# Identity matmuls on TensorE in five early waits of a cross-attention and expert-FFN kernel

## What is computed

```python
x = x + xattn(layernorm(x), ctx, pos, pos, Wq, Wkv, Wout, bout)
x = x + ffn(layernorm(x), gate_w, bias, shared_w1, shared_w3, shared_w2, w1, w3, w2)

# xattn: 32 heads of 16
q = (x @ Wq).reshape(b, n, 32, 16)
k, v = split(ctx @ Wkv, 2)
q, k = apply_axial_rope(q, pos), apply_axial_rope(k, pos)
w = softmax(einsum('bqhd,bkhd->bhqk', q, k) * 16 ** -0.5)
return einsum('bhqk,bkhd->bqhd', w, v).reshape(b, n, 512) @ Wout + bout

# ffn: one shared expert, and the best 2 of 16 routed experts, inner width 352
shared = (silu(x @ w1.T) * (x @ w3.T)) @ w2.T
routed = sum over e of combine[:, e] * (silu(x @ w1[e].T) * (x @ w3[e].T)) @ w2[e].T
```

## Time and profile before

| | us |
|---|---|
| three runs | 683.81, 691.29, 691.58 |
| their median | 691.29 |
| profiled execution, first to last instruction | 686.8 |
| TensorE busy in it | 635.5 |

### The profile page before, as it was taken

How to read it: one execution, slowest core, us unless ns; L and a number is a source line. 1 busy time by engine, 2 the same in 40 slices (tenths; PEclk the granted TensorE clock), 3 DMA queues, 4 the chain that set the end, 5 groups by cost and what they waited for, 6 DMA issues and landing times.

```text
span 686.8 us, 19435 instructions
## 1 busy us (share of the span) xinstructions
PE 635.5 (93%) x7104; PEld 406.1 (59%) x7104; DVE 503.7 (73%) x976; ACT 368.5 (54%) x620; POOL 329.9 (48%) x390
## 2 busy tenths in 40 slices
PE   2779999999999999988999999999997999999992
PEld 0255666666666666656566566666664666666661
DVE  8688888888888899866485935676775676666671
ACT  4255655656566665566411115665764666666660
POOL 3434555555555555432000011467666577767562
PEclk9889999999999999999999999999999999999997
DMA  8934755344444445660322563676778855555952
GB/s 291 247 56 62 173 103 94 88 97 99 99 99 99 99 99 122 94 125 33 115 86 76 204 220 92 173 219 98 209 211 257 229 115 92 92 88 150 246 92 33
DMA packets 105296, 90.63 MB, mean 132 GB/s; under 512 B 71649, under 2 KB 75745, under 8 KB 105249
## 3 DMA queue, kind: packets, MB, share of 16 engines
q1 hardware_dynamic: 91872, 60.28, 34.2%
q0 software_dynamic: 8752, 20.71, 16.2%
q10 hardware_dynamic: 4624, 9.00, 4.0%
HBM read 69.85 MB, written 22.81 MB: 135 GB/s over the span
## 4 chain that ended last, share of the span: by engine, by line
PE 76%; DMA 7%; issue 4%; POOL 3%; ACT 3%; DVE 3%; SPq 1%; POOLq 0%; ACTq 0%; DVEq 0%
PE p_sc L725 14%; PE p_qk L694 13%; PE p_sc L694 12%; PE p_qk L505 8%; PE p_v L505 8%; PE p_pv L594 4%; DMA used_twice_too<-used_twice 3%; PE p_pv L597 3%; PE p_tr L688 2%; PE p_pv L712 2%; PE p_sc L553 2%; PE p_pv L604 2%; PE p_sc L574 2%; PE p_sc L577 1%; SPq L426 1%
## 5 line engine op out<-in xcount | busy, mean ns | idle before, releaser
L1088 DVE TENSOR_REDUCE negmax<-p_sc 128x4 f16<-128x512 f32 x128 | 79.4, 683 | 6.8 <-PE p_sc L553 5.4
L934 ACT CAST hiddenT<-p_pv 128x384 f16<-128x384 f32 x54 | 25.8, 478 | 106.0 <-PE p_pv L712 102.2
L812 ACT ACTIVATE prob<-p_sc 128x512 f32<-128x512 f32 x128 | 66.1, 604 | 20.7 <-PE p_sc L577 20.4
L1494 POOL DMA_INDIRECT out<-prob,to_at x38 | 68.2, 1796 | 10.1 <-issue 8.2
L725 PE MATMUL p_sc<-used_twice,hiddenT 128*128 128x512 f16 (+1 forms) x306 | 71.6, 379 | 0.9 <-DVE hiddenT L1218 0.9
L1474 POOL COPY from_at<-from_rows 128x1 uint32 (+1 forms) x40 | 32.3, 808 | 80.8 <-DVE from_rows L1333 77.4
L694 PE MATMUL p_qk<-used_twice,xeT 128*128 128x352 f16 x420 | 68.4, 313 | 0.6 <-DMA xeT<-xn2T_dram 0.6
L694 PE MATMUL p_sc<-used_twice,xeT 128*128 128x352 f16 x420 | 68.4, 312 | 0.0
L1214 DVE TENSOR_TENSOR hidden<-p_sc,act_g 128x352 f32<-128x352 f32 x55 | 28.8, 524 | 52.5 <-PE p_sc L694 32.1
L921 ACT COPY xeT<-p_tr 128x1024 f16<-128x1024 f16 x40 | 40.5, 1012 | 37.2 <-PE p_tr L688 35.6
L505 PE MATMUL p_qk<-used_twice,xnT 128*128 128x512 f16 x192 | 53.1, 405 | 5.3 <-DVE swp L1066 5.3
(11 more groups left out here) (180 smaller groups left out, 1482.3 us busy)
## 6 DMA issues: line engine op xcount, KB each, us to landing
w<-e SPq DMA_DIRECT2D x20, 1408.0 KB
w<-e SPq DMA_DIRECT2D x20, 512.0 KB
out<-stream SPq DMA_DIRECT2D x17, 256.0 KB, 2.0
xn_dram<-xn_parts SPq DMA_DIRECT2D x16, 256.0 KB, 2.2
xn2T_dram<-xn2T SPq DMA_DIRECT2D x16, 256.0 KB, 2.5
w<-e SPq DMA_DIRECT2D x20, 192.0 KB
xeT<-xn2T_dram ACTq DMA_DIRECT2D x14, 256.0 KB, 2.8
stream<-x ACTq DMA_DIRECT2D x1, 3072.0 KB, 16.8
```

The lines of the kernel that those rows point to most:

```text
L812: act.activation(prob[:, c % RING, :], p_scored(c)[:], ACT.Exp, scale=SCALE).then_inc(exp_ready, 1)
L1088: dve.tensor_reduce(negmax[:, c % 2, at:at + CH], p_scored(c)[:].rearrange("p (h t) -> p h t", t=P), AX_X, ALU.max, negate=True).then_inc( ...
L1494: pool.indirect_dma_start(out=out, out_offset=bass.IndirectOffsetOnAxis(ap=to_at[:, par, u:u + 1], axis=0), in_=ye[:, par, u], in_offset=N ...
```

## The change

TensorE gets a helper `keep_busy(n)`, which issues n matmuls with the fp16 identity as the stationary operand and the same identity, repeated four times, as 512 moving columns. They write the whole of `p_pv`, and nothing reads the result. They wait for no semaphore of their own and signal none. Eight of them stand ahead of the very first transposes, behind the wait for `ident_ready`. Others stand at places in the step function that a table `BUSY` names by step and place: 14, 15, 8, 9 and 9. The table is looked up only for steps with a constant number, so the loop's body stays as it was.

```diff
+            def keep_busy(n):
+
+                for _ in range(n):
+                    pe.matmul(p_pv[:], ident16[:], ident16[:].rearrange("p (o t) -> p o t", o=1).broadcast_to([P, CH, P]), start=True, stop=True)
+
+            BUSY = {(0, "before k"): 14, (1, "before q"): 15, (2, "before q"): 8, (2, "before scores"): 9, (3, "before shift"): 9}
+
+            def fill(b, where):
+
+                if isinstance(b, int):
+                    keep_busy(BUSY.get((b, where), 0))
+
             pe.wait_ge(ident_ready, 1)
+            keep_busy(8)
             xn_transpose(0, 0)
...
                 on(-1, project_k, 1)
+                fill(b, "before shift")
                 on(-3, negmax_transpose)
...
+                fill(b, "before q")
                 on(-1, project_q, 0)
                 on(-3, spread_recip, 0)
                 on(-1, project_q, 1)
+                fill(b, "before scores")
                 on(-2, scores, 0)
...
                 on(0, xn_transpose)
+                fill(b, "before k")
                 on(0, project_k, 0)
```

## The result

The change made the kernel slower. Over 20 runs of each, its median is 694.92 us (690.61 to 701.88) against 690.33 us before (683.81 to 694.93). The ratio is 1.0092, 95% interval [1.0065, 1.0118], so some 6 us. The ratios in this document are taken over the fast runs of each kernel, those within 1.5% of its fastest. My forecast was 688.5 us, 2.8 us under the 691.29 us of the three runs known then, and its range ended at 692.

The account below looks back on a forecast made before the run. TensorE, busy 635.5 of 686.8 us, was taken as the bound, so only the start could gain: 1.0 (transposes) + 1.8 (step 2) + 0 (shifted scores) = 2.8 us off the 691.3 median gives 688.5 us, range 681 to 692.

Parts of the forecast that it names:

- The clock: At TensorE's start: the added matmuls raise the clock by 11.3 us, so that q of batch 0 runs fast.
- The case in which the four transposes don't count: Start: transpose-mode work doesn't raise the clock, which rises near 12.4 us; q starts 0.7 us late, the sum loses 0.1.
- What the slow pace cost: Slow matmuls at the start: at most 2.06 us shows for q of batch 0, 1.88 in step 2, shifted scores 0 to 0.9.
- what is late next: After q of batch 0: busy DMA passes on only 1.0 of 2.06 us; step 2 then gives 1.8.
- the transposes' term: DMA transposes of batch 0's q: an earlier q half queues behind k's, so scores gain 1.0 us, between 0 and 2.06.
- that of step 2: Step 2's scores, q half and v chunk at the fast pace: 1.88 us less some 0.1 for row maxima, 1.8.
- The 4.5 us by which I set the median over the profiled execution: Whole kernel: the three-run median 691.3 us lies 4.5 us over the profiled 686.8; if that spread stays, the forecast is 688.5.
- A shift should survive: the order is fixed, and from some 140 us on TensorE is full: Whole kernel behind the start: time gained there, 2.8 us, moves everything later forward and lasts to the end.
- the term for the added matmuls: TensorE's early waits: each added matmul costs 0.215 or 0.427 us; hidden at the fast pace, partly over at the slow.
- The slower one: From q of batch 0 on: identity matmuls don't raise the clock and delay work by 9.3 us, to 700.6 us; chance 0.05.
- Absorbed: Scores still wait for DMA transposes until 31.7; the end moves at most 1 us, to 690.3 to 691.3; chance 0.18.
- The spread's rival: Start: run-to-run spread is the clock's and the change removes it, giving 684.0 us, or 681.0 from the best run; chance 0.20.

Follow-up runs that it names:

- e9: e8 run again unchanged (the change plus 65 matmuls of 16 columns, 128 added in all), against the kernel before: ratio 0.9938, median 684.79 us.
- e10: e8's code with all 128 added matmuls at 16 columns, against the kernel before: ratio 0.9974, median 686.43 us.
- e1: The kernel before once more with no edit, as a second sample against the kernel before: ratio 0.9974.
- e5: The kernel before with 63 matmuls of 16 columns added in TensorE's first wait, against the kernel before: ratio 1.0108.
- e6: The kernel before with 128 matmuls of 16 columns added in TensorE's first wait, against the kernel before: ratio 0.9961.
- e4: The change with only the groups of steps 2 and 3 (8, 9, 9), against the kernel before: ratio 1.0007.
- e2: The change with its 63 added matmuls at 16 columns in place of 512, against the kernel before: ratio 1.0102, median 699.28 us.
- e11: The kernel before with 191 matmuls of 16 columns in its first three waits, against the kernel before: ratio 1.0065.
- e8: The change plus 65 matmuls of 16 columns in its own waits, 128 added in all, against the kernel before: ratio 0.9930, median 686.41 us.
- e3: The change with only the groups ahead of the first transposes, k and q (8, 14, 15), against the kernel before: ratio 1.0027.
- e7: The kernel before with 32 matmuls of 16 columns added in TensorE's first wait, against the kernel before: ratio 1.0012.
- e12: The change plus 33 matmuls of 16 columns in its waits, 96 added in all, against the kernel before: ratio 0.9979.

## Why the prediction was wrong

**The clock, right.** The identity matmuls raised it. The clock rose even before the 11.3 that I worked out: all 14 ahead of k are fast in the changed kernel. In e9's profile they took 4.62 us, so part of them was slow there, and the 25 small ones behind them made k start at 12.27: the moment at which the clock rises varies between executions. So does it without them: q of batch 0 took 5.23 us in one profile of the kernel before and 4.36 in the other. The case in which the four transposes don't count, with the clock up near 12.4, was met in neither profile.

**What the slow pace cost, and what is late next: right in the sum, wrong in both terms.** q of batch 0 was to run from 16.8 to 19.4 and ran from 16.68 to 19.27, where the next product starts. VectorE took it up at 19.82 (20.0 said), the scores began at 29.91 (29.7 to 31.7), the v copy was 2.57 us earlier (2.8), and the clock held from 28 to 46 us, as the row of that stretch says (length; busy us and instructions of PE, PEld, DVE, ACT, POOL; granted clock; DMA):

```profile
28.00:46.00 18.00, 13.61 (x200) 7.80 (x197) 14.71 (x29) 10.83 (x19) 6.30 (x5) 1.00 0.60 73
```

The DMA transposes gave back 1.82 us of q's 2.06, where I took 1.0; step 2 gave only some 0.8 more, since the second halves of the transposes came into its way (a wait of 0.95 at 33.52). The sum, 2.8 us, measured 2.58 in this profile and 2.8 between e9 and e10. That it fits is in good part luck: the transposes' term was 0.8 us too low and that of step 2 1.0 us too high, and the split isn't stable either. Between e9 and e10 the scores start only 0.1 us apart (31.98 and 32.10), and step 2 gives the other 2.7. And the profile before is itself one of several: against e1's the lead is 1.36 us.

The 4.5 us by which I set the median over the profiled execution compare a run's time with a span. A run's time is its span and 1.9 us, so the distance was 2.6.

**"A shift should survive: the order is fixed, and from some 140 us on TensorE is full": this step failed**, and with it the term for the added matmuls. I priced them by their time on the array alone, 0.215 or 0.427 us each, and called them hidden. That is right for the array. They are also 126 instructions of code, and these I put at nothing without a reason; but an order that is fixed can still lie elsewhere in its packets. Half a packet of shift costs 1.0092 / 0.9938 = 1.0155 by the change against e9, and 1.0108 / 0.9961 = 1.0148 by e5 against e6: 10 us, four times the gain.

Where these lie, by e5 against e6 (profiles of 697.5 and 685.8 us): up to the first transposed maxima 0.1 us (42.2 and 42.1); from there to the last ones 269.7 against 266.7, 3.0 us; to the 18th hidden transposes 132.1 against 129.1, 3.0 us; the rest 253.4 against 248.0, 5.4 us. In the loop, where there is at most one fetch, nothing is lost: from the 6th to the 14th transposed maxima each of the fourteen profiles takes 141.2 to 141.3 us, e4 alone 141.7. In the first two stretches waits for DMA work grow: those for transposes sum to 8.7 us in e5 and 3.8 in e6 (with the one ahead of the first maxima, 3.4 and 2.5), those for token rows to 3.3 and 0.9.

```profile
PE p_sc L553 <- DMA used_twice_too<-used_twice: 8.7, 8, 3.4
...
PE p_qk L696 <- DMA xeT<-xn2T_dram: 3.3, 3, 1.9
```

```profile
PE p_sc L553 <- DMA used_twice_too<-used_twice: 3.8, 4, 2.5
...
PE p_qk L696 <- DMA xeT<-xn2T_dram: 0.9, 1, 0.9
```

The waits for token rows are three in the change, e2, e5 and e11 alike, and one or two in all the others. A fetch is near only one of the three: in each of the four kernels the second wait has a 16 KB packet 2.6 to 2.7 us before its end, while its load is under way. The third, which is the longest (0.9 to 3.2 us), has none: the last such packet went 9.6 to 11.9 us before its end, ahead of the load's issue. So the place brings this wait about, but not by a fetch beside the load.

The third stretch goes with the place too. The same three stretches in all fourteen profiles, in us:

```
place   first to last maxima   to the 18th hidden   the rest         profiles
0       264.6 to 266.9         128.6 to 129.3       246.8 to 250.4   before, e1, e6, e8, e9, e10
1/4     266.6 to 268.0         128.8 to 129.0       252.2 to 258.6   e3, e4, e7
1/2     267.7 to 270.6         130.4 to 135.8       250.6 to 253.4   change, e2, e5, e11
3/4     268.6                  132.2                251.7            e12
```

In the rest, TensorE waits 3.3 to 4.2 us at a time for gathered rows: once or twice in each of the eight profiles that are off place 0, and in one of the six at place 0, the first of the kernel before. The wait costs more than its own length where the clock falls behind it. In e5 it is 3.7 us and ends at 514.9, and the stretch from 516 to 520 has 12 matmuls at a granted clock of 0.50, where the next has 30:

```profile
516.00:520.00 4.00, 4.00 (x12) 1.75 (x11) 0.10 (x1) 0.96 (x1) 2.17 (x4) 0.50 0.55 201
520.00:524.00 4.00, 4.00 (x30) 2.71 (x29) 2.90 (x4) 3.57 (x6) 2.39 (x5) 0.97 0.69 131
```

**The rivals.** The slower one ended on the right side by the wrong mechanism: it wanted q at 22.4, and q started at 16.68. "Absorbed" would have held for the profiled execution up to 307 us, but not for the cause: the lead wasn't absorbed by transposes that are late anyway, but lost to transposes that had become later. The spread's rival was wrong: with a fast start the runs of the change still spread over 11 us. The sentence of the Trainium skill that this rival leans on stands in "TensorE: Matmul & The Clock Gate", Part 1, under "What's actually happening", and not under Terms; its under 1%, here 6.9 us, agrees with the 6.8 us to which the slow pieces of the profile before add up.

**Open.** That the place costs the 10 us is shown by the runs. How it does is shown in part: a fetch delays a transpose by e5's first case and by the count, not by a run without fetches. Why places 1/4 and 3/4 cost little and 1/2 a lot is not shown; which transposes and loads are critical may be a matter of each case. For the waits for gathered rows no fetch can be named: none of those over 3 us has a 16 KB packet between the load's issue and the wait's end. They also come and go between runs of one kernel, there is one profile of each, and those of e3 and e7 lie well over their kernels' medians (697.5 and 694.73 us, against 691.94 and 690.84); so that the place makes them more frequent rests on the eight against one of six. And e6, e8, e9 and e10 all lie below 1, e6 and e10 by 0.3 to 0.4% without any part of the clock, though the place of the later code is that of the kernel before; their intervals just reach 1. None of the four profiles has the long wait for gathered rows, and one of the two of the kernel before has. That would fit, but isn't shown.

## What to carry to other kernels

An instruction costs its engine's time and also its place in the code: on an engine with long straight-line code, adding or removing instructions anywhere moves every later instruction fetch, and here half a packet of shift was worth 10 us of 690, more than what the edit was for. A step that counts new instructions by their time on the engine alone leaves this term out. Before an edit is judged by 1%, run the same code length with the work taken out (16 columns in place of 512), and the edit padded to a whole packet: the pair tells the edit's worth from that of the place. Keeping TensorE's clock up through the first waits moves the start 1.4 to 2.8 us ahead by the profiles here, a gain that the run times alone don't tell from nothing; padded to 128 matmuls it gives the fastest kernel of this study, 0.993 of the time before.

## What the runs showed of the hardware

- TensorE's instructions come in DMA packets of 16 KB (31 in this kernel), one for 249 to 260 instructions on average in straight-line code; 128 added matmuls made it 32.
- A DMA transpose with such a packet under way between issue and landing took 4.28 us on average against 3.22 without (199 and 401 of them). A packet of 8 KB of the other instruction queue did nothing (3.19 us, 13 of them).
- Behind a wait of 3.7 us at 514.9 in e5 the granted clock was 0.50 from 516 to 520; behind one of 3.5 us at 532.1 in the kernel before it stayed at 1.00.
- The clock rises on matmuls with an identity on both sides: the first 8 took 3.59 us, the 14 behind them 3.18 us.
- A matmul of 16 columns takes little time: 63 with their weight loads were done in 1.85 us, where I had allowed 3.
